# A graph network on one core: packed step words, unpacked in registers, and arrival counts read four at a time

## The reference, cut to what matters

```python
h = relu(layernorm(x));  x = x + L0(h)     # 3 graph convolutions
h = relu(layernorm(x));  x = x + L1(h)     # 2 graph attention layers

# L0, three times
h = h * out_norm[:, None]
h = segment_sum(h[src], dst) * in_norm[:, None]
h = h @ W[i] + b[i]                        # relu but for the last

# L1, twice: 4 heads of 64, loops added to the edges
h = (x @ W).reshape(n, 4, 64)
alpha = leaky_relu(a_src[src] + a_dst[dst])
e = exp(alpha - segment_max(alpha, dst)[dst])
w = e / clip(segment_sum(e, dst), 1e-16)[dst]
out = segment_sum(w[:, :, None] * h[src], dst) + bias
```

## Time and profile before

| | us |
|---|---|
| median of three runs | 6946.7 (6940.96 to 6950.69) |
| the profiled execution's own time | 6875.32 |
| its span | 6873.5 |
| mean granted TensorE clock, share of full speed | 0.71 |

### The profile page before, as it was taken

How to read it: one execution, slowest core, us unless ns; L and a number is a source line. 1 busy time by engine, 2 the same in 40 slices (tenths; PEclk the granted TensorE clock), 3 DMA queues, 4 the chain that set the end, 5 groups by cost and what they waited for, 6 DMA issues and landing times. The chain is left out here.

```text
span 6873.5 us, 84355 instructions
## 1 busy us (share of the span) xinstructions
PE 4202.8 (61%) x14997; PEld 2812.5 (41%) x14997; DVE 3621.6 (53%) x12180; ACT 2136.3 (31%) x7094; POOL 4130.3 (60%) x4276
## 2 busy tenths in 40 slices
PE   8555555565555556555555636666666556666774
PEld 7333333343333334333333424444444334444442
DVE  6444444544444444444444636666666556666667
ACT  4000000020000002000000247677777467767774
POOL 7666666366666664666666356566664556666663
PEclk7666666776666668666666867777778777777776
DMA  3333333133333332333333233333333323333334
GB/s 100 95 95 89 91 91 91 55 103 90 91 89 91 90 90 85 90 91 90 91 91 90 85 112 88 87 90 89 88 90 86 104 77 89 88 89 87 89 89 133
DMA packets 309602, 625.46 MB, mean 91 GB/s; under 512 B 85343, under 2 KB 180411, under 8 KB 309080
## 3 DMA queue, kind: packets, MB, share of 16 engines
q0 software_dynamic: 192928, 530.18, 27.7%
q1 hardware_dynamic: 109800, 88.51, 4.1%
q10 hardware_dynamic: 6384, 1.39, 0.1%
HBM read 573.23 MB, written 47.33 MB: 90 GB/s over the span
## 5 line engine op out<-in xcount | busy, mean ns | idle before, releaser
L1127 PE MATMUL main<-ring,oh 128*128 x4992 | 2039.7, 573 | 1582.9 <-DVE oh L1413 775.2
L695 POOL DMA_INDIRECT ring<-conv_tab,csrc x2346 | 2221.4, 947 | 1232.7 <-issue 613.0
L1421 DVE TENSOR_TENSOR acc<-acc,main 128x264 f32 (+2 forms) x4160 | 1762.7, 424 | 1964.9 <-PE main L1127 688.1
L1127 PEld LDWEIGHTS main<-ring,oh 128*128 128x128 f32 x4992 | 1337.3, 286 | 2282.1 <-issue 2038.2
L707 POOL DMA_INDIRECT ring<-attn_tab,sidx x1664 | 1586.1, 953 | 1079.4 <-issue 441.2
L1230 PE MATMUL main<-ring,oh 128*128 128x264 f32 x3328 | 1367.9, 528 | 354.8 <-ACT ring L959 190.5
L1413 DVE TENSOR_SCALAR oh<-iota,dloc 128x128 f32<-128x128 f32 x2505 | 765.0, 306 | 474.1 <-issue 327.2
L959 ACT ACTIVATE ring<-ring 128x64 f32<-128x64 f32 x3328 | 906.5, 340 | 0.0
L1230 PEld LDWEIGHTS main<-ring,oh 128*128 128x128 f32 x3328 | 672.9, 247 | 546.0 <-issue 349.0
L937 ACT ACTIVATE oh<-iota,dloc 128x128 f32<-128x128 f32 x1664 | 527.2, 391 | 2.7 <-DMA attn_tab<-oh 2.7
L1766 DVE TENSOR_TENSOR ring<-ring 128x128 f32<-128x128 f32 x1664 | 463.6, 284 | 0.0
(11 more groups left out here) (215 smaller groups left out, 3012.1 us busy)
## 6 DMA issues: line engine op xcount, KB each, us to landing
ring<-conv_tab,csrc POOLq DMA_INDIRECT x2346
ring<-attn_tab,sidx POOLq DMA_INDIRECT x1664
ring<-attn_tab SPq DMA_DIRECT2D x14, 896.0 KB, 8.2
conv_tab<-oh SPq DMA_DIRECT2D x12, 896.0 KB, 4.0
flag_room<-start_rows SPq DMA_DIRECT2D x416, 8.0 KB
flag_room<-end_rows SPq DMA_DIRECT2D x416, 8.0 KB
x_tab<-acc SPq DMA_DIRECT2D x7, 896.0 KB
oh<-x_tab SPq DMA_DIRECT2D x7, 896.0 KB
```

The lines of the kernel that those rows point to most:

```text
L695: pool.indirect_dma_start(ring3[:, c % U, 0:C], None, conv_tab[k], bass.IndirectOffsetOnAxis(ap=csrc[:, c:c + 1], axis=0)).then_inc(gather ...
L1127: nc.tensor.matmul(main[s % 4][:, 0:width], oh[:, (s % OHR) * P:(s % OHR + 1) * P], ring[:, bass.ds(slots[s % 8], width)], start=True, sto ...
L1421: nc.vector.tensor_tensor(a, a, main[k][:, 0:width], ALU.add).then_inc(added, 1)
```

## The change

Two tables take the place of `step_tab`'s four rows. The arrival counts stay one 16-bit word a step and are read four at a time. Slot and tile (not their columns) of four steps share one 32-bit word of a row each, six bits a step. An engine reads four such words for sixteen steps, and shifts, masks and multiplies a register at each use. The slot word is read every sixteen steps of a convolution. The table is packed on VectorE in the preparation, and two tables are written and read back by SyncE. ScalarE's DMAs for the neighbour keys and flags are wrapped in a function that is called in the same order, on one semaphore instead of two.

```diff
-        step_words = dram("step_words", (4, SX), U16)
+        arrival_words = dram("arrival_words", (1, SX), U16)
+        step_words = dram("step_words", (2, SX // 4), I32)
...
-        ARRIVALS, SLOT_AT, SUMS_AT, LOGITS_OF = range(4)
-        LAST_AT = (EC, (U - 1) * AW, (NT - 1) * AW, (NT - 1) * LW)
-
-        def step_values(engine, row, s, n):
+        ARRIVALS, SLOT, TILE = range(3)
+        FIELD = 64
+
+        def step_words_of(engine, row, s):
 
             return nc.values_load_multi_w_load_instructions(
-                step_tab[row:row + 1, s:s + n], engines=[engine], min_val=1 if row == ARRIVALS else 0, max_val=LAST_AT[row],
-                skip_runtime_bounds_check_because="chunk, slot and tile are clamped on the chip")[1]
+                step_tab[row - 1:row, s // 4:s // 4 + G // 4], engines=[engine], min_val=0, max_val=FIELD ** 4 - 1,
+                skip_runtime_bounds_check_because="four fields of six bits, each clamped on the chip")[1]
+
+        def field(words, k, width, most):
+
+            word = words[k // 4] >> (6 * (k % 4)) if k % 4 else words[k // 4]
+            part = nc.s_assert_within(word & (FIELD - 1), 0, most, skip_runtime_bounds_check_because="clamped on the chip")
+            return part * width
+
+        def sums_of_step(words, k):
+            return field(words, k, AW, NT - 1)
+
+        def arrivals_of(engine, s):
+
+            return nc.values_load_multi_w_load_instructions(
+                arrival_tab[0:1, s:s + 4], engines=[engine], min_val=1, max_val=EC,
+                skip_runtime_bounds_check_because="chunk counts are clamped on the chip")[1]
...
             sp.wait_ge(words_ready, 2)
-            sp.dma_start(step_words.rearrange("w (b p) -> (w b) p", p=P), step_rowsT).then_inc(words_in, 16)
-            sp.wait_ge(words_in, 16)
+            sp.dma_start(arrival_words.rearrange("w (b p) -> (w b) p", p=P), arrival_rowsT).then_inc(words_in, 16)
+            sp.dma_start(step_words.rearrange("w (b p) -> (w b) p", p=P // 4), step_rowsT[SB:3 * SB, :]).then_inc(words_in, 16)
+            sp.wait_ge(words_in, 32)
+            sp.dma_start(arrival_tab, arrival_words).then_inc(words_in, 16)
             sp.dma_start(step_tab, step_words).then_inc(words_in, 16)
...
                 for s in range(0, S):
-                    if s % 8 == 0:
-                        counts = step_values(mybir.EngineType.PE, ARRIVALS, s, 8)
-                        slots = step_values(mybir.EngineType.PE, SLOT_AT, s, 8)
+                    if s % G == 0:
+                        slots = step_words_of(mybir.EngineType.PE, SLOT, s)
+                    if s % 4 == 0:
+                        counts = arrivals_of(mybir.EngineType.PE, s)
...
-                    pe.wait_ge(arrived[k], counts[s % 8])
+                    pe.wait_ge(arrived[k], counts[s % 4])
...
-                                     ring[:, bass.ds(slots[s % 8], width)], start=True, stop=True).then_inc(products_done, 1)
+                                     ring[:, bass.ds(field(slots, s % G, AW, U - 1), width)], start=True, stop=True).then_inc(products_done, 1)
...
-                    return step_values(mybir.EngineType.PE, LOGITS_OF, g * G, G)
+                    return step_words_of(mybir.EngineType.PE, TILE, g * G)
...
-                                          tvb[:, bass.ds(tiles[j], LW)], start=True, stop=True)
+                                          tvb[:, bass.ds(field(tiles, j, LW, NT - 1), LW)], start=True, stop=True)
...
-            link(nc.vector.tensor_copy(col[SLOT_AT], cslot))
             link(nc.vector.tensor_scalar(col[ARRIVALS], cs, 1.0, None, ALU.add))
-            link(nc.vector.tensor_scalar(col[SUMS_AT], tsc, float(AW), None, ALU.mult))
-            link(nc.vector.tensor_scalar(col[LOGITS_OF], tsc, float(LW), None, ALU.mult))
-            nc.vector.tensor_scalar(col[SLOT_AT], col[SLOT_AT], float(AW), None, ALU.mult).then_inc(words_ready, 1)
+            link(nc.vector.tensor_copy(col[TILE], tsc))
+            nc.vector.tensor_copy(col[SLOT], cslot).then_inc(words_ready, 1)
             hist(3, 4)
             dve.wait_ge(words_T, 1)
-            nc.vector.tensor_copy(step_rowsT, psb[0:4 * SB, P:2 * P]).then_inc(words_ready, 1)
+            four = psb[0:3 * SB, P:2 * P].rearrange("r (j k) -> r k j", k=4)
+            nc.vector.tensor_copy(arrival_rowsT, psb[0:SB, P:2 * P])
+            link(nc.vector.tensor_scalar(step_low, four[:, 1, :], float(FIELD), None, ALU.mult))
...
+            nc.vector.tensor_tensor(step_rowsT, step_high, step_low, ALU.add).then_inc(words_ready, 1)
...
-                    if s % 8 == 0:
-                        sums_at = step_values(mybir.EngineType.DVE, SUMS_AT, s, 8)
+                    if s % G == 0:
+                        sums_at = step_words_of(mybir.EngineType.DVE, TILE, s)
...
-                    accumulate(sums_at[s % 8], s % 4, C + 1 if k == 0 else C, k * S + s)
+                    accumulate(sums_of_step(sums_at, s % G), s % 4, C + 1 if k == 0 else C, k * S + s)
...
-                        sums_at = step_values(mybir.EngineType.DVE, SUMS_AT, (it * GB + b) * G, G)
+                        sums_at = step_words_of(mybir.EngineType.DVE, TILE, (it * GB + b) * G)
...
-                            a4 = acc[:, bass.ds(sums_at[0], C)].rearrange("p (h c) -> p h c", h=H)
+                            a4 = acc[:, bass.ds(sums_of_step(sums_at, 0), C)].rearrange("p (h c) -> p h c", h=H)
...
-                            accumulate(sums_at[k], k % 4, AW, s0 + k)
+                            accumulate(sums_of_step(sums_at, k), k % 4, AW, s0 + k)
```

More of the change, by code:

```diff
@@ L802, in _, with neighbour_keys @@
             copy_projected(NT - 1)
-            act.wait_ge(keys_ready, 1)
-            nc.scalar.dma_start(keys[0:1, 1:1 + SX * P].rearrange("o (b p e) -> (o p) b e", p=P, e=P),
-                                key[:, :, 1:P + 1]).then_inc(key_out, 16)
-            with nc.allow_non_contiguous_dma(reason="one element of each step"):
-                act.wait_ge(key_out, 16)
+            def neighbour_keys(s):
                 kv = keys[0:1, 0:SX * P].rearrange("o (b p e) -> (o p) b e", p=P, e=P)
-                nc.scalar.dma_start(key[:, :, 0:1], kv[:, :, 0:1]).then_inc(key_out, 16)
@@ L817, in _ @@
-                nc.scalar.dma_start(end_any.rearrange("o (b p) -> (o p) b", p=P), eany).then_inc(flags_out, 16)
-                act.wait_ge(flags_out, 64)
+                with nc.allow_non_contiguous_dma(reason="one element of each step"):
+                    if s == SROW_AT:
+                        act.wait_ge(keys_ready, 1)
+                        nc.scalar.dma_start(keys[0:1, 1:1 + SX * P].rearrange("o (b p e) -> (o p) b e", p=P, e=P),
+                                            key[:, :, 1:P + 1]).then_inc(key_out, 16)
+                    if s == SROW_AT + 8:
+                        act.wait_ge(key_out, 16)
+                        nc.scalar.dma_start(key[:, :, 0:1], kv[:, :, 0:1]).then_inc(key_out, 16)
+                        nc.scalar.dma_start(key[:, :, P + 1:P + 2], kn[:, :, P - 1:P]).then_inc(key_out, 16)
+                    if s == EROW_AT + 56:
+                        act.wait_ge(flags_ready, 1)
+                        nc.scalar.dma_start(start_rows.rearrange("(b p) e -> p b e", p=P), b3(sfr)).then_inc(key_out, 16)
+                        nc.scalar.dma_start(end_rows.rearrange("(b p) e -> p b e", p=P), b3(efr)).then_inc(key_out, 16)
+                        nc.scalar.dma_start(start_any.rearrange("o (b p) -> (o p) b", p=P), sany).then_inc(key_out, 16)
+                        nc.scalar.dma_start(end_any.rearrange("o (b p) -> (o p) b", p=P), eany).then_inc(key_out, 16)
+                    if s == S - 1:
+                        act.wait_ge(key_out, 112)
@@ L1369, in _ @@
                 scale_rows(q)
-            dve.wait_ge(words_in, 32)
+            dve.wait_ge(words_in, 64)
             dve.wait_ge(rowsT_read, KB)
```

30 lines of the change are left out of this document (17 added, 13 removed).

## The result

The changed kernel takes 7040.75 us (median of 4 runs, 7033.59 to 7046.12), the kernel before in the same session 6945.32 (4 runs, 6940.96 to 6950.69). The ratio is 1.0143, 95% interval 1.0129 to 1.0157: slower by 1.4%. Forecast were 6210 us and a range of 5880 to 6600.

What follows compares the result with a forecast made beforehand. Register loads on TensorE and VectorE were taken to hold GpSimd's gathers above their floor. From 6875 us profiled, -480 for convolutions, -255 for attention and +1 for preparation gave 6141, times 1.0104 about 6210 us; range 5880 to 6600.

Steps and rivals of the forecast that it cites:

- Price of a load: Register loads on TensorE and VectorE: a load of four, 16-bit or 32-bit words alike, takes 0.98 and 0.95 us.
- Price of a field: Unpacking one value at each use costs 0.18 us on VectorE and 0.2 on TensorE, only the multiply fused.
- Convolution block without stretches: Eight convolution steps of the changed kernel take about 7.0 us when no slow register instructions disturb them.
- stretches: Convolutions: TensorE register and semaphore instructions take up to 1394 ns, raising the mean block from 9.06 to 11.49 us.
- The factor 1.27: Convolutions: slow stretches multiply a block, 7.0 to 8.9 us, 9.95 with GpSimd; three passes lose 480 us.
- Attention: Both loads come off each attention group fully, 17 fields add 3.0 us: 24.45 to 22.0 us, -255 us in all.
- Preparation: Packing on VectorE and a second table written and read by SyncE cost about +1 us.
- The factor from profiled execution to median: Whole kernel: the shown median is 1.0104 times the profiled time, turning 6141 us into 6205.
- E: Rival: shift and mask on VectorE's path are dear, breaking even near 0.6 us a field; 7490 us, chance 0.06.
- C: Rival: slow stretches follow instructions issued, about 25% more on TensorE in convolutions; +67 us a pass, 6410 us, chance 0.09.
- A: Rival: GpSimd is all that is left, with fused unpacking or cheap 32-bit loads; 5875 us, chance 0.20.

Runs made afterwards that it cites:

- short loads: Kernel before with arrival counts as four 16-bit words a load, other step values as four 32-bit words, nothing unpacked: 6755.69 us, 0.9848 of before.
- one wait in four: short loads, with TensorE waiting for arrivals only at every fourth convolution step: 6740.94 us, 0.983 of before.
- the pass-by-pass kernel: short loads changed in each pass alone; attention with the old long load on TensorE in its first pass, VectorE in its second: 6786.47 us, 0.99 of before.
- the paced kernel: short loads and one wait in four, with GpSimd slowed by memsets of 8 columns behind gathers: 6324.95 us, 1.1258 of before.

## Why the prediction was wrong

- **Price of a load.** The counts of four, 0.98 forecast, 0.985 measured; 884 loads on TensorE and 260 on VectorE, right. Four 32-bit words were taken at 0.98 and 0.95 and cost 0.33 and 0.34, near the lower bound of 0.28: words of 16 bits pay for each word, four adjacent words of 32 did not. The Trainium skill ("DMA: Bandwidth & Descriptors", Latency and other measured facts) has a floor of about 600 ns under a register load; the trace has 334. The Trainium skill's 200 ns a register ("Runtime: NRT & Kernel Launch", Instruction fetch mechanics) is near the 16-bit words, 985/4 = 246, and far from these, 334/4 = 84. The error was in the change's favour.
- **Price of a field.** 0.18 us on VectorE and 0.2 on TensorE, with shift and mask separate and the multiply fused. Found: exactly this split, about 0.15 us on VectorE between wait and sum. Right.
- **Convolution block without stretches.** 7.0 us forecast. The few blocks of eight steps in the changed kernel's trace without a slow instruction, 14 or 15 of 103 a pass, take 6.6 in the median. Before has 51 to 57 of them, at 8.5 in the median, so the 9.06 that the factor was taken from, one block, was on the long side. Right in kind.
- **The factor 1.27, the step that failed.** "So about 7.0 us without slow stretches, and x 1.27 = 8.9 us with them", and 9.95 with GpSimd. A stretch is no tax on each block. It lasts until GpSimd has made up its lead and stops; shorter loads on TensorE gain nothing before the tail, since the gathers of 1.25 us set the pace and only the stops come on top. The stops stay at 158 to 162 us a pass with long loads, short loads and one wait in four, and go to 226 with unpacking. A pass became 978 + 226 + a tail of 53, less some 10 before the first sum, 1246 us, not 1035. Forecast -480, found +156.
- **Attention.** -2.64 - 2.80 us a group for the two loads, since "each stands in the chain". Both did stand in it, but cutting them shortened it little: TensorE's load is worth nothing and VectorE's 10 us a pass, as the pass-by-pass kernel shows. That the other side of the loop would have come almost as late in each place is my reading; no run shows it. The changed kernel's chain has the same hole for "issue" as the earlier trace rows, though TensorE's load is now 0.33 us:

```profile
6092.25 0.64 PE main L1259 x2
6092.89 3.24 issue
6096.13 1.22 PE main L1259 x2
```

  The fields took back more than that: 1254 with short loads, 1278 in the changed kernel. Forecast -255, found +13.
- **Preparation.** Nothing, +1 us; the time outside the passes went from 747.5 to 742.8. Right. The factor from profiled execution to median, 1.0104, did not carry over: it is 1.0005 for the changed kernel.
- **The rivals.** Slower had 0.07, nearly all of it for E, a dear register operation, that decides from 0.6 us a field. The field is 0.15; the mechanism was wrong. C came nearest: the pass does grow with TensorE's instructions. But the slow intervals grew by only 13 us a pass over short loads (640 to 653), the others by 55. It was priced at +67 us a pass on top of a gain that wasn't there; on the passes of before that +67 would have been near the +52 found, for a reason that is only in part C's. A, GpSimd as all that is left, is what happens without stretches, for both kernels alike: 5621 and 5629.
- **What could have been read.** The idle of 1232.7 us before the gathers, less 704, is 529 us of stops in three passes. The blocks of loads come 104 times a pass; of the stops of before 64 to 66 a pass are over 1 us long and 39 or 40 over 2. The stop of 2.84 us before 1018.78 falls between two pairs of loads and was not the loads' doing. I took the two as one limit and let the loads pay for both.

What stays open: what makes the stretches, and why the sum waits so long for a product whose matmul is on record. They were there in four sessions (before at 6858 to 6957 us) and absent in three (5617 to 5621); a chip of the same number is listed once with them and once without, which speaks for the moment more than for the chip, but the list does not prove that it is one chip. They need gathers in unbroken sequence: half of them took nearly all stretches away. Whether it is the pace, the descriptors or the semaphore traffic of the gathers was not separated, as the paced kernel met no stretches. Why the end of the gathers ends one, and not the time, is inferred from their order in the traces.

## What to carry to other kernels

Before pricing what a waiting engine saves, write a pass as the floor of its slowest fixed-rate engine plus that engine's stops, and ask of each edit which stop it removes; here 3.9 us of loads every eight steps removed none. Subtract a group's own gap (0.30 us a gather) from its idle row and count what is left: floor, stops and tail together gave the length of a convolution pass in every kernel of this study. And a disturbance that takes a quarter of the time must not be carried along as a factor: take it away or double it in an experiment first, and measure in more than one session.

## What the runs showed of the hardware

- A register load of four adjacent 32-bit words takes 0.33 us on TensorE and 0.34 on VectorE; four 16-bit words 0.985 to 0.992.
- Shift and mask on a register are single instructions (36 ns on TensorE, 45 on VectorE), not fused with the multiply and add (46 and 57 ns).
- An indirect gather of 128 rows occupies GpSimd for 0.947 us and is followed by 0.30 us in which one wait and a memset of 8 columns cost nothing, and a second pair costs 0.6 us. Neither the bytes nor the wait before it changes the 1.25.
- In a disturbed session a part of the register and semaphore instructions of TensorE, and of VectorE where it unpacks, take about 0.7 us, a few 1.4, instead of 0.04; some 30 of SyncE's 2380 semaphore instructions do, GpSimd's don't. Products come 3.3 to 3.5 us apart: with one arrival wait in four, 1145 of 2496 sums start over 1.5 us after the product's matmul record ends, against 8 in an undisturbed session. The DMA packets take the same time in all.
